# The last stage of a transformer step on one Trainium2 core, with its instructions in another order

## The reference

```python
q = (x @ W_q.T)                                  # 4 heads, two halves each
sim = einsum('pbthn,hkpn->pbthk', q, keys)       # 64 x-similarities and 64 y-similarities per head
scores_xy, idx_xy = top_k(sim, 8)                # the best 8 of each half
all_scores = sx[..., :, None] + sy[..., None, :] # 64 sums of pairs
scores, pk = top_k(all_scores, 8)                # the best 8 pairs, each pair is one of 512 experts
w = silu(einsum('btd,bthkd->bthk', x, de) * softmax(scores))
experts = einsum('bthk,bthkd->btd', w, ue)
dense = silu(x @ W_up.T) @ W_down.T
out = x_in + dense + experts
```

## Time and profile before

| | before |
|---|---|
| median of 3 runs | 506.21 us (505.69 to 508.18) |
| the profiled execution, its own time | 505.62 us |
| its span, first to last instruction | 503.9 us |
| busy, share of the span: PE / DVE / ACT / POOL | 413.8 (82%) / 346.2 (69%) / 311.9 (62%) / 310.3 (62%) us |
| mean granted TensorE clock | 0.878 of full speed |

### The profile page before, as it was taken

The page is one execution under the profiler, slowest core; times in us unless marked ns, Lnnn a source line. Parts: engine busy times, 40 slices in busy tenths (PEclk is TensorE's granted clock), DMA queues, the critical chain, the costliest instruction groups (busy, mean ns, idle before and its releaser), DMA issues.

```text
span 503.9 us, 8841 instructions
## 1 busy us (share of the span) xinstructions
PE 413.8 (82%) x2400; PEld 330.9 (66%) x2400; DVE 346.2 (69%) x1359; ACT 311.9 (62%) x792; POOL 310.3 (62%) x236
## 2 busy tenths in 40 slices
PE   4897888755999944969655899999998989989876
PEld 3786777624998943859422676777676766767666
DVE  3457777611232214798688999999999999899831
ACT  1443537241122212698743889899898998989845
POOL 5135867871000027573039789999989898998940
PEclk9577959776999995595777699999999999999999
DMA  6982000102576611120000000100001010100000
GB/s 197 354 222 79 33 21 22 43 31 62 153 222 198 179 42 53 35 86 27 1 10 1 21 23 32 33 31 21 10 31 31 31 31 31 31 31 21 12 12 21
DMA packets 42165, 31.84 MB, mean 63 GB/s; under 512 B 3899, under 2 KB 38299, under 8 KB 42139
## 3 DMA queue, kind: packets, MB, share of 16 engines
q1 hardware_dynamic: 38283, 24.95, 16.8%
q0 software_dynamic: 2624, 6.30, 3.7%
q10 hardware_dynamic: 1232, 0.31, 0.3%
HBM read 18.95 MB, written 8.39 MB: 54 GB/s over the span
## 4 chain that ended last, share of the span: by engine, by line
DVE 19%; ACT 14%; PE 11%; issue 7%; DVEq 1%; POOL 0%; ACTq 0%; POOLq 0%
ACT arena_sb L798 6%; DVE arena_sb L1623 6%; PE banks L1193 4%; DVE arena_sb L1601 3%; PE banks L1147 2%; PE banks L1202 2%; ACT L821 2%; DVE banks L1549 2%; DVE first_sb L1544 2%; DVE best_sb L1594 1%; PE banks L1178 1%; ACT banks L761 1%; ACT w_t_sb L559 1%; DVE first_sb L1564 1%; ACT summed_sb L812 1%
## 5 line engine op out<-in xcount | busy, mean ns | idle before, releaser
L523 POOL TENSOR_TENSOR arena_sb<-arena_sb 128x2144 f32<-128x2144 f32 x31 | 146.8, 4752 | 5.7 <-DVE arena_sb L1623 5.3
L1623 DVE SCALAR_TENSOR_TENSOR arena_sb<-arena_sb,best_sb,banks 128x536 f32<-128x536 f32 x124 | 87.4, 768 | 5.0 <-issue 2.5
L798 ACT ACTIVATE arena_sb<-arena_sb,bsum_sb 128x536 f32<-128x536 f32 x124 | 81.7, 733 | 0.2
L481 POOL DMA_INDIRECT arena_sb<-made,made_row_sb x32 | 30.9, 967 | 79.2 <-DMA made<-arena_sb 70.3
L513 POOL TENSOR_TENSOR arena_sb<-ex_sb,ey_sb 128x2048 f32<-128x2048 f32 x16 | 58.0, 3625 | 17.4 <-ACT banks L771 13.2
L1193 PEld LDWEIGHTS banks<-ident_sb,arena_sb 128*128 128x128 f32 x496 | 58.2, 153 | 13.0 <-ACT summed_sb L812 9.5
L1193 PE MATMUL banks<-ident_sb,arena_sb 128*128 128x128 f32 x496 | 61.5, 278 | 4.2 <-ACT summed_sb L812 4.2
L1147 PE MATMUL banks<-z_sb,xt_sb 128*128 128x512 f32 x64 | 37.0, 677 | 12.2 <-DVE arena_sb L1601 10.6
L1202 PE MATMUL banks<-up_e_sb,w_t_sb 128*128 128x128 f32 x256 | 35.4, 281 | 9.3 <-ACT w_t_sb L559 9.3
L1202 PEld LDWEIGHTS banks<-up_e_sb,w_t_sb 128*128 128x128 f32 x256 | 32.2, 191 | 13.2 <-ACT w_t_sb L559 12.4
L1433 DVE TENSOR_SCALAR arena_sb<-banks 128x512 f32<-128x512 f32 x16 | 11.1, 692 | 39.2 <-PE banks L1043 39.2
(11 more groups left out here) (189 smaller groups left out, 868.8 us busy)
## 6 DMA issues: line engine op xcount, KB each, us to landing
arena_sb<-w SPq DMA_DIRECT2D x32, 256.0 KB, 3.5
x_all_sb<-x SPq DMA_DIRECT2D x8, 256.0 KB, 3.3
slots<-arena_sb POOLq DMA_DIRECT2D x4, 512.0 KB, 8.5
arena_sb<-slots SPq DMA_DIRECT2D x16, 128.0 KB, 3.1
made<-arena_sb SPq DMA_DIRECT2D x16, 128.0 KB, 1.9
xt_sb<-x_t_sb SPq DMA_DIRECT2D x16, 128.0 KB, 2.0
xu_sb<-x_t_sb SPq DMA_DIRECT2D x16, 128.0 KB, 2.0
out<-x_all_sb SPq DMA_DIRECT2D x16, 128.0 KB, 1.8
```

The source lines that it names most:

```text
L523: pool.tensor_tensor(prod[r][p], prod[r][p], table[r][p][:, :, 0:WIDE], ALU.mult).then_inc(weighed, 1)
L798: ins = act.activation(prod[r][p][:, h, :], prod[r][p][:, h, :], ACT.Silu, scale=bsum[r][:, n:n + 1])
L1623: ins = dve.scalar_tensor_tensor(out=prod[r][p][:, h, :], in0=table[r][p][:, h, 0:WIDE], scalar=best[r][:, n, TOP - 1:TOP], in1=scores_of( ...
```

## The change

Nothing is computed in another way; helpers are called in another order.

- ACT, `turn`: `list_exps(i+1)` now stands before `weights_out(i-1, 0)`.
- PE, `turn`: `keys(i+2, 0)` moves from behind `down` to between `scores(i+1, 0)` and `up(i, 0)`; `keys(i+2, 1)` stays. `back(i, 0)` moves from behind both `add_experts` to between them.
- DVE, `turn`: `norms(i+1)` moves from before `pick(i+1, 0)` to behind `tops(i+2)`.
- Start: `pool_tile` is 1 for pair 1 too, so POOL makes the table of its tile 1 and VectorE that of its tile 0; the waits of `y_exps` and `keys` follow this. (`norms` is also written a second time with the same text.)
- End: ACT's helpers of pairs 14 and 15 stand in another order, and `result(NP-3)` on DVE is called inside `last_pick`, in front of the two picks into banks.

```diff
@@ pool_tile
-            return 1 if i is FIRST else 0
+            return 1 if isinstance(i, int) and i < 2 else 0
@@ act, y_exps
-                if past(i, 1) and p == 0:
+                if past(i, 1) and p == pool_tile(i):
                     act.wait_ge(table_ready, i)
@@ act, turn
                 y_exps(i + 1, 0)
+                list_exps(i + 1)
                 if past(i, 1):
                     weights_out(i - 1, 0)
-                list_exps(i + 1)
                 y_exps(i + 1, 1)
@@ act, end
             turn(NP - 2, 0, more=1)
+            silus(NP - 2, 0, 1)
             weights_out(NP - 2, 0)
-            silus(NP - 2, 0, 1)
+            tail(NP - 2, 0, 1)
             hidden(NP - 1, 0)
-            tail(NP - 2, 0, 1)
+            silus(NP - 1, 1, 0)
             hidden(NP - 1, 1)
+            tail(NP - 1, 1, 0)
             weights_out(NP - 2, 1)
-            silus(NP - 1, 1, 0)
-            tail(NP - 1, 1, 0)
@@ pe, keys
                 if past(i, 1):
                     pe.wait_ge(ey_ready, 2 * i - 2 + p + 1)
-                if past(i, 2) and p:
-                    pe.wait_ge(own_ready, i)
-                elif isinstance(i, int) and i == 1 and not p:
-                    pe.wait_ge(own_ready, 1)
+                    if p != pool_tile(i - 1):
+                        pe.wait_ge(own_ready, i)
@@ pe, turn
-                if more:
-                    scores(i + 1, 1 - r, 0)
+                scores(i + 1, 1 - r, 0)
+                if more == 2:
+                    keys(i + 2, r, 0)
                 up(i, r, 0)
-                if more:
-                    scores(i + 1, 1 - r, 1)
+                scores(i + 1, 1 - r, 1)
                 if past(i, 1):
                     down(i - 1, 0)
                     down(i - 1, 1)
                 if more == 2:
-                    keys(i + 2, r, 0)
                     keys(i + 2, r, 1)
                 if past(i, 1):
                     back(i - 1, 1 - r, 1)
                 up(i, r, 1)
                 if past(i, 1):
-                    add_experts(i - 1, 0, more > 0)
-                    add_experts(i - 1, 1, more > 0)
+                    add_experts(i - 1, 0)
                 back(i, r, 0)
+                if past(i, 1):
+                    add_experts(i - 1, 1)
@@ dve, last_pick and turn
                 ins.then_inc(late_picked, 1)
+                result(NP - 3)
                 dve.wait_ge(picked_ready, NT - 1)
...
                 own_table(i + 1, 1 - r)
-                norms(i + 1, 1 - r)
                 pick(i + 1, 1 - r, 0)
                 if more == 2:
                     tops(i + 2)
+                norms(i + 1, 1 - r)
...
             last_pick()
-            result(NP - 3)
```

More of the change, by code:

```diff
@@ L1633, in norms @@
                 dve.reciprocal(bsum[r][:, :], bsum[r][:, :]).then_inc(norm_ready, 1)
+            def norms(i, r):
+                dve.wait_ge(best_ready, i + 1)
+                if past(i, 2):
+                    dve.wait_ge(silu_ready, 2 * i - 2)
+                step(dve.tensor_reduce(bsum[r][:, :], best[r][:, :, :], AXX, ALU.add))
+                dve.reciprocal(bsum[r][:, :], bsum[r][:, :]).then_inc(norm_ready, 1)
             def last_pick():
```

## The result

| | before | changed |
|---|---|---|
| median | 506.1 us (505.69 to 508.18, 4 runs) | 516.32 us (515.65 to 517.03, 4 runs) |
| ratio to before | | 1.0203, 95% interval 1.0174 to 1.0233 |
| profiled execution, own time / span | 505.62 / 503.9 us | 516.99 / 515.3 us |
| mean granted TensorE clock | 0.878 | 0.891 |

The kernel became 2% slower, 11.4 us in the profiled spans. To see where, I take four landmarks on VectorE, which every version has: the starts of `own_table` of pairs 1, 2 and 15 and of the last `result`. The columns are differences of these starts in the timelines, each from the one profiled execution of its kernel. Before, the turns of the loop alternate between about 13.45 and 14.86 us in the steady part, and 14.09 is their mean; now each takes 14.66 to 14.72.

A forecast was written before the change was run, and what follows sets the result against it. The prediction took DVE's work to bound the loop before, and a chain over DVE, PE and ACT after. Loop +7.0, start +3.6, last turn +1.2, end -1.8 gave +10.0 us; it named 515.8 us, range 510.5 to 519.5.

The forecast's parts named there:

- The cycle in the loop: Loop: closed chain from pick(i, 1) through DVE, PE and ACT to pick(i+1, 1), 14.6 us per turn, +7.0 us.
- the signs that the forecast named: Loop: turns 14.5 to 14.7 us, pick(.., 1) waits 0.6 to 1.1, norms none, PE over 1 at keys.
- What bounded the kernel before: Loop before the change: bound by DVE's work, 13.33 us of a 14.07 us turn, other waits costing little.
- the forecast's 13.73: Loop: us per turn of the kernel before if DVE's 4.3 us of norms waits were gone.
- list_exps counts nothing: Loop: POOL's table starts up to 1.54 us earlier, but POOL is not the bound, so no gain.
- The start: Start: keys(2, 0) waits for DVE's table ahead of scores(1, 1) on PE, delaying pick(1, 0): +3.6 us.
- The last turn and the end: Turn 14 repeats the loop's chain, +1.2 us; the reordered end then gives -1.8 us.
- The tokens' load: Loop: tokens for the earlier keys(i+2, 0) land 4.5 us after issue's reference, PE arrives after some 5.4: nothing.
- The gap: Rival, loop: norms stops waiting, DVE's work alone sets the turn, 503.1 us, or 500.1 with full clock at start; chance 0.08.
- The cheap start: Rival, start: PE's clock at full speed there, 512.8 us; chance 0.15.
- The branch: Rival, loop: DVE's 0.5 us branch comes after PE's result, six turns grow, +3.0, 518.8 us; chance 0.12.
- The start and the end: Rival: no effect in the loop, only start and end count, about 508 us; chance 0.05.

The follow-up runs named there:

- e1: Changed kernel with back(i, 0) again behind both add_experts on PE: 506.07 us, ratio 1.0005 to before.
- e2: Kernel before with back(i, 0) between the two add_experts as the only edit: 518.35 us, ratio 1.0243.
- e9: Changed kernel with two unused 128x256 sums on VectorE behind norms: 519.68 us, one run.
- e10: Changed kernel with two unused 128x256 sums on VectorE directly in front of own_table: 526.21 us, one run.
- e12: Kernel before with list_exps and weights_out(i-1, 1) earlier, the changed end, and back(i, 0) between the two add_experts: 520.3 us, ratio 1.0279.
- e11: Kernel before with two unused 128x256 sums on VectorE behind tops: 509.61 us, one run.
- e4: Kernel before with norms(i+1) behind tops(i+2) on VectorE as the only edit: 507.79 us, ratio 1.0046.
- e5: Kernel before with list_exps(i+1) ahead of weights_out(i-1, 0) as the only edit: 503.32 us, ratio 0.996.
- e6: Kernel before with ACT's weights_out(i-1, 1) moved from behind tail(i, 0) to ahead of hidden(i, 1): 500.16 us, ratio 0.9885.
- e7: Kernel before with list_exps earlier, weights_out(i-1, 1) ahead of hidden(i, 1), and the changed kernel's order at the end: 497.65 us, ratio 0.9845.
- e3: Changed kernel with keys(i+2, 0) put back directly ahead of keys(i+2, 1): 515.62 us, ratio 1.0202.
- e8: Changed kernel with two unused 128x256 products on VectorE behind norms: 601.96 us, one run.

## Why the prediction was right

**The sign and the size** were right: forecast 515.8 us, range 510.5 to 519.5, measured 516.32. The closeness is in part luck. Between the two profiled executions the forecast was +10.0 and it was +11.4: the loop cost 0.9 us more than forecast, the last turn and the end 0.9 more, and what comes ahead of the stage was 0.35 faster. The median lies 0.7 us below the profiled execution of the changed kernel, where it had stood 0.6 above that of the kernel before. (The forecast's own sum gives 515.6 + 0.6 = 516.2, not 515.8.)

**The cycle in the loop.** Forecast 14.6 us per turn and +7.0; measured 14.70 and +7.9. The mechanism is shown: undoing the split removes it (e1), the split alone makes it (e2), load off it is free and load on it counts in full (e9, e10). Of the signs that the forecast named, `norms` without a wait, PE's wait of over 1 us at `keys` and the even turns came; `pick(.., 1)` waits 1.2 to 1.3 us, more than the 0.6 to 1.1 named. The 0.1 us are latencies and one length: `back(i, 0)` starts 0.13 behind the tail's end (401.06 + 0.20, to 401.39) where I took 0.07, and takes 1.80 instead of 1.75 after a wait. It was found from a wait that the profile did not show: `pick` had been just in time. The order of calls and the semaphore's count had to be read for it.

**One link of the cycle** was read incompletely. The forecast goes from `keys` through `back(i-1, 1)` and `up(i, 1)` on PE to `hidden` on ACT. There is a second way from `keys` to `hidden`, on ACT alone: `nears` waits for `keys` (1.24 us), the four SiLUs stand behind it, `hidden` behind those. In the turn shown `up` ends at 400.34 and `hidden` starts at 400.41, when ACT comes from the SiLUs without a gap; the profile's chain of last-ending work takes this way and not PE's. Both were within 0.07 us of each other before, too (`up` ends at 393.04, `hidden` starts at 393.11 behind the SiLUs), and the change moved neither against the other, so the sum was right by luck in this link. e12 is the run in which ACT's way grew alone: `hidden` starts at 402.02 there, and its `up` had ended at 401.47. A faster `back` or `up` by itself would then gain next to nothing; no run tests that.

**What bounded the kernel before** was stated wrongly, though it did not matter for the sum. I named DVE's work, with `norms`' wait as the only loss. e11 and e4 contradict: extra work on DVE costs a seventh of itself (0.09 of 0.65 us), and taking the wait from `norms` gives it to the next instruction. e5 and e6 point to the cause, the places of `list_exps` and of the evictions in ACT's queue: moving one eviction took away PE's waits for it and DVE's waits in `norms` together. Only in e6 and e7 does DVE wait for no engine, at 13.74 and 13.69 us a turn; the forecast's 13.73 for that state was the right length from a wrong reading.

**list_exps counts nothing** was wrong. Alone it gains 0.2 us a turn (e5), because ACT does not stand behind `back` with the exponentials queued. In the changed kernel the cycle should hide this gain; no run takes this edit out of it.

**The start.** Forecast +3.6, measured +3.5 between the `own_table` of pairs 1 and 2. For the earlier trace rows:

```profile
280.49 2.82 DVE L1621 SCALAR_TENSOR_TENSOR arena_sb<-arena_sb,best_sb,banks 128x536 f32<-128x536 f32 x4 [5.71 <-ACT banks L782]
```

```profile
274.93 2.05 PE L1145 MATMUL banks<-z_sb,xt_sb 128*128 128x512 f32 x2 [8.48 <-DVE arena_sb L1599]
276.77 1.91 PE L1165 MATMUL banks<-xu_sb,w_up_t_sb 128*128 128x256 f32 x4
278.47 1.59 PE L1151 MATMUL banks<-down_t_sb,xt_sb 128*128 128x512 f32 x2
```

The pick waits for `lates`, this for `scores(1, 1)`, this for `keys(2, 0)`. `keys` and `up` took the half-clock times; `scores` took 1.59 us, between 2.05 and 1.02, and the granted clock was 0.50 from 278 to 279 us, 0.70 in the next one and 1.00 from 280 to 282, so the clock rose during it, as the rule of the Trainium skill ("TensorE: Matmul & The Clock Gate", "What you observe") had allowed. Counted from the table's end, the pick itself was 3.06 us later than before, where the forecast had 3.6. The rest of the 3.5 is the work behind it, where `norms` now stands in front of `pick(1, 1)` (0.45), which the forecast had left out: the two errors cancel by luck.

**The last turn and the end.** Forecast +1.2 and -1.8, measured together +0.3 behind `own_table(15)`. This step failed. Most of its terms came. The last turn cost +0.7 instead of +1.2 (the first of `last_pick` starts 13.29 us behind `pick(14, 1)`, 477.90 to 491.19, before 12.61). `down(14, 0)` began 3.26 us after it (491.19 to 494.45), as forecast (3.2). The wait in front of `back(14, 1)` is gone, and the one before the second `add_experts(14)` is 0.91 us instead of 0.28. But the forecast took it that PE's calls there keep their durations. PE had idled 0.72 and 1.58 us shortly before, and:

```profile
494.45 3.58 PE L1176 MATMUL banks<-w_down_t_sb,h_sb 128*128 128x128 f32 x16 [1.58 <-DVE banks L1645]
497.81 2.04 PE L1191 MATMUL banks<-ident_sb,arena_sb 128*128 128x128 f32 x16
```

```profile
494.00:496.00 2.00, 1.55 (x8) 1.58 (x9) 1.68 (x3) 0.00 (x0) 1.32 (x2) 0.66 0.23 65
496.00:498.00 2.00, 2.00 (x11) 2.00 (x11) 0.00 (x0) 0.00 (x0) 0.00 (x0) 0.50 0.00 0
```

The granted clock fell to 0.50, 1.2 GHz, and `down` took 3.58 us instead of 2.02. That took back 1.6 us of the gain. In e1, with the same order at the end and the clock at 1.00, the end took 27.50 us, 2.3 less than before; in e7 27.11.

The waits alone do not decide it. e3 and e9 have the same two waits there (0.72 and 1.57) and `down(14)` at 3.48 and 3.52 us. e10 has them too, at a granted clock of 1.00:

```profile
503.59 2.02 PE L1176 MATMUL banks<-w_down_t_sb,h_sb 128*128 128x128 f32 x16 [1.58 <-DVE banks L1645]
```

There the clock fell only for the `down` of pair 15 (3.55 us), behind waits of 0.99 and 0.60. What decides between the two, the traces do not show.

**The tokens' load** cost one wait of 0.4 us in the loop, nothing as forecast.

**The rivals.** The gap did not close: DVE's wait moved to `pick`, and even on the kernel before, the edit that closes it gained nothing (e4). The cheap start did not come, though the clock went part of the way. The branch did not add up: it vanished in the wait for PE, and all 13 turns are 14.66 to 14.72. The start and the end did not decide alone.

## What to carry to other kernels

A wait that the profile doesn't show may be one that is met to the last tenth; before an instruction is moved down a queue, look up every semaphore that counts it, and walk from its waiter back to itself. If that closes, the new period is at least the walk's length, however little the engines have to do, and every way that is as long counts, here one on PE and one on ACT. Where an engine waits for an eviction, move the eviction up on its own engine (e6, -1.1%) before pushing other work in front of the waiting call (e2, +2.4%). And a gap that a small instruction shows need not be its own: e4 moved it, and the next instruction waited instead.

## What the runs showed of the hardware

Two SBUF-to-SBUF products of 128x256 on VectorE, beside GpSimd's products of 128x2048 and 128x2144, took 1.27 and 3.83 us, and a turn grew by 5.8 us (e8), while one of them took 0.41 us with GpSimd idle, and two sums of 128x256 in the same place 0.37 and 0.41 (e9). And behind waits of 0.72 and 1.6 us between PE's bursts the granted clock went to 0.50 at the end of the changed kernel, of e3 and of e9, and not in e10; the loop of the changed kernel, with a wait of 1.17 and one of 0.41 us per turn, stayed at 1.00 from 300 us on.
